# A gated cross-attention block on one core: layer norm on an input transposed by the host, and work moved from VectorE to ScalarE

## The reference

```
q = layernorm(x); k = v = ctx                       # 256 x 512
gates = [q, k, v] @ [igate_kernel, fgate_kernel] + bias   # 8 input, 8 forget gates a token
per head (8 heads of 64): D from cumulated log-sigmoid of the forget gates and a running maximum,
   C = (q @ k.T / 8) * D, h = C / (max(|sum C|, exp(-max)) + eps) @ v, then an RMS norm
x = x + tanh(g_xattn) * h
t = layernorm(x)                                    # second norm
g, u = bitlinear(t, w_gate), bitlinear(t, w_up)     # 2048 wide, tokens and weights quantised
x = x + tanh(g_ffn) * bitlinear(relu(g)**2 * u, w_down)
```

## Time and profile before

| | |
|---|---|
| median of 3 runs | 602.35 us (601.4 to 603.7) |
| the profiled execution | 605.11 us, its span 603.4 us |
| PE busy | 578.3 us, 96% |
| DVE busy | 526.2 us, 87% |
| ACT busy | 453.1 us, 75% |
| POOL busy | 129.9 us, 22% |
| granted TensorE clock, mean | 0.986 |

### The profile page before, as it was taken

The page is one execution under the profiler, slowest core; times in us unless marked ns, Lnnn a source line. Parts: engine busy times, 40 slices in busy tenths (PEclk is TensorE's granted clock), DMA queues, the critical chain, the costliest instruction groups (busy, mean ns, idle before and its releaser), DMA issues.

```text
span 603.4 us, 18384 instructions
## 1 busy us (share of the span) xinstructions
PE 578.3 (96%) x6571; PEld 339.0 (56%) x6571; DVE 526.2 (87%) x1150; ACT 453.1 (75%) x926; POOL 129.9 (22%) x284
## 2 busy tenths in 40 slices
PE   7986779999999999999999999999999999999996
PEld 3744435656565655656565655656565655655452
DVE  3799897998989898998989898998989898997964
ACT  4799888686876868686886869687786868687661
POOL 3267142120311212120211213120221213120100
PEclk9999879999999999999999999999999999999998
DMA  9959050050605023050504023050504114020100
GB/s 315 382 194 316 28 174 21 23 189 4 211 0 190 20 92 117 18 192 0 210 0 172 37 77 132 18 192 0 197 12 143 66 43 168 20 89 1 37 18 35
DMA packets 44114, 62.68 MB, mean 104 GB/s; under 512 B 1849, under 2 KB 25649, under 8 KB 44081
## 3 DMA queue, kind: packets, MB, share of 16 engines
q1 hardware_dynamic: 44080, 62.24, 29.6%
HBM read 53.72 MB, written 8.51 MB: 103 GB/s over the span
## 4 chain that ended last, share of the span: by engine, by line
PE 81%; ACT 8%; DVE 5%; issue 4%; POOL 1%; DMA 1%; SPq 0%; DVEq 0%; ACTq 0%; POOLq 0%
PE yb L1230 17%; PE gb L1204 17%; PE ub L1204 16%; PE tp L1251 8%; PE ab L1238 7%; PE ab L1218 4%; PE tp L1278 3%; PE ab L1261 3%; PE ab L1239 2%; ACT wdT L528 1%; ACT wgT L536 1%; POOL stage L446 1%; PE ab L1312 1%; DVE stage L810 1%; DMA xs<-in_x 1%
## 5 line engine op out<-in xcount | busy, mean ns | idle before, releaser
L1204 PE MATMUL gb<-wgT,xqT 128*128 128x512 bf16 x512 | 133.6, 384 | 0.0
L1204 PE MATMUL ub<-wuT,xqT 128*128 128x512 bf16 x512 | 132.6, 382 | 0.5 <-DVE stage L810 0.3
L1230 PE MATMUL yb<-wdT,stage 128*128 128x512 bf16 x512 | 124.0, 387 | 4.2 <-ACT stage L558 4.2
L544 ACT ACTIVATE relu<-gb 128x512 f32<-128x512 f32 x128 | 75.3, 588 | 45.9 <-PE gb L1204 45.5
L810 DVE TENSOR_TENSOR stage<-relu,ub 128x512 f32<-128x512 f32 x128 | 86.9, 679 | 16.2 <-ACT relu L546 16.2
L1204 PEld LDWEIGHTS ub<-wuT,xqT 128*128 128x128 bf16 x512 | 49.5, 98 | 63.5 <-DVE stage L810 4.8
L546 ACT ACTIVATE relu<-relu 128x512 f32<-128x512 f32 x128 | 80.8, 631 | 4.1
L937 DVE SCALAR_TENSOR_TENSOR dmat<-ab,dmat 128x384 f32<-128x384 f32 x128 | 65.1, 550 | 19.3 <-POOL dmat L454 13.3
L1230 PEld LDWEIGHTS yb<-wdT,stage 128*128 128x128 bf16 x512 | 47.8, 99 | 54.6 <-issue 5.0
L1204 PEld LDWEIGHTS gb<-wgT,xqT 128*128 128x128 bf16 x512 | 46.1, 101 | 45.4 <-issue 1.9
L454 POOL TENSOR_SCALAR_AFFINE_SELECT dmat<-dmat 128x256 f32<-128x256 f32 x128 | 55.7, 463 | 59.5 <-ACT dmat L604 46.8
(11 more groups left out here) (131 smaller groups left out, 893.7 us busy)
## 6 DMA issues: line engine op xcount, KB each, us to landing
dmat<-max_rows SPq DMA_DIRECT2D x15, 1024.0 KB, 5.1
values<-in_ctx_v SPq DMA_DIRECT2D x16, 520.0 KB, 7.6
xs<-in_x SPq DMA_DIRECT2D x16, 512.0 KB, 5.9
cT<-in_ctx_t SPq DMA_DIRECT2D x16, 512.0 KB, 6.9
out<-stage SPq DMA_DIRECT2D x32, 256.0 KB, 2.0
stage<-in_w_gate SPq DMA_DIRECT2D x4, 1024.0 KB, 12.1
stage<-in_w_up SPq DMA_DIRECT2D x4, 1024.0 KB, 13.5
stage<-in_w_down SPq DMA_DIRECT2D x4, 1024.0 KB, 7.1
```

Source lines behind the costliest of these rows:

```text
L544: nc.scalar.activation(relu[:, c % 2, :], gb[c % 2][:, :], ACT.Relu).then_inc(g_free, 1)
L1204: last = nc.tensor.matmul(bank[c % 2][:, :], xqT[par][:, t, d, :], w[:, d, c * CH:(c + 1) * CH], start=(d == 0), stop=(d == KD - 1))
L1230: done = nc.tensor.matmul(yb[:, :], hqT[:, c, :], wdT[:, c, :], start=(c == 0), stop=(c == KF - 1))
```

## The change

Before, x was normalised on VectorE (two tensor_scalar), transposed on TensorE (eight transposes) and copied to `qT` on ScalarE. Now the host also hands over x transposed, and one more transfer of 512 KB a batch (`turned`) puts it into `qT`. Means and reciprocal deviations lie one to a partition; TensorE transposes each of the four columns, broadcast to 128 x 128, into the bank `yb`, so that every partition there holds them as rows (`stat_rows`), and VectorE subtracts and multiplies them in place (`norm_rows`, four tensor_tensor). Batches 0 and 1 keep the old way. Since `yb` is in use, `down(b-1, 1)` now starts only after `norm_rows`.

The token centres of the second norm (x2 less its mean, now with the sign turned) go from VectorE to ScalarE, before the rstd operations. The second half of both evictions of quantised hidden transposes goes from VectorE to ScalarE in the steps from 1 to 13; `hidden(b, 1, 1)` moves ahead of the token maxima. For the last batch `down` is made in two halves of 256 columns, with two outputs and two stores, and in the last step the hidden maximum of tile 1 is split after 2 chunks instead of 3. Eight more matmuls keep TensorE busy in the prologue.

```diff
+            def turned(n, par):
+                sp.dma_start(qT[par][:, :, :], x_t[bass.ds(n, 1), :, :].rearrange("o (k p) s -> p (o k) s", p=P)).then_inc(xt_in[par], 16)
             def load(n, par):
                 for t in range(T):
                     sp.wait_ge(x2_ready[t], n - 1)
                 queries(n, par)
+                turned(n, par)
...
+            def token_centres(n, npar):
+                act.wait_ge(ln2_step, LN2_K * n + 4)
+                for t in range(T):
+                    nc.scalar.activation(xm[:, t, :], x2[npar][:, t, :], ACT.Identity, scale=-1.0,
+                                         bias=mv2[:, t, 0:1]).then_inc(centred, 1)
...
@@ ScalarE, the steps @@
+                    hidden_cols(b - 1, 1, 1)
                 if n is not None:
                     heads(n, 3)
                     squares(n)
-                if m is not None:
-                    for t in range(T):
-                        columns(m, qT[par], t)
                 quantise_high(b, 0)
...
+                    token_centres(n, npar)
                     tokens_rstd(n)
                 if m is not None:
                     hidden_cols(b, 0)
+                if prev and m is not None:
+                    hidden_cols(b, 0, 1)
...
@@ VectorE @@
+            def norm_rows(m, par):
+                dve.wait_ge(rows_full, m - 1)
+                dve.wait_ge(xt_in[par], turned_loads(m, par))
+                halves = [qT[par][:, :, t * P:(t + 1) * P] for t in range(T)]
+                for t in range(T):
+                    mean_row = yb[:, None, t * P:(t + 1) * P].to_broadcast([P, KD, P])
+                    nc.vector.tensor_tensor(halves[t], halves[t], mean_row, ALU.subtract).then_inc(q_step, 1)
+                for t in range(T):
+                    rstd_row = yb[:, None, S + t * P:S + (t + 1) * P].to_broadcast([P, KD, P])
+                    dve.wait_ge(q_step, 2 * m - 3 + t)
+                    nc.vector.tensor_tensor(halves[t], halves[t], rstd_row, ALU.mult).then_inc(q_ready, 1)
...
-                    attention_norm(m, par)
+                    norm_rows(m, par)
                 hidden_max(b, 0, 0)
                 if not prev:
                     magnitudes(2, 3)
                 hidden(b, 0, 3)
-                if prev and n is not None:
-                    hidden_cols(b - 1, 1)
...
                     scale_weight(2, 2)
                 elif m is not None:
                     hidden(b, 1, 0)
-                if n is not None:
-                    token_centres(n, npar)
+                if prev:
+                    hidden(b, 1, 1)
+                if n is not None:
+                    token_maxima(n)
                 if not prev:
                     scale_weight(2, 3)
+                if n is not None:
+                    quantise_tokens(n)
+                if n is None:
+                    hidden_max(b, 1, 0, NC // 2)
+                if not prev or m is None:
+                    hidden_cols(b, 0)
+                hidden(b, 1, 2)
+                if m is not None:
+                    negated_max(m)
+                if n is not None:
+                    hidden_max(b, 1, 0)
+                hidden(b, 1, 3)
+                if n is not None:
+                    hidden_max(b, 1, 1)
                 else:
-                    hidden(b, 1, 1)
-                if n is not None:
-                    quantise_tokens(n)
-                hidden_cols(b, 0)
-                hidden(b, 1, 2)
-                if m is not None:
-                    negated_max(m)
-                hidden_max(b, 1, 0)
-                hidden(b, 1, 3)
-                hidden_max(b, 1, 1)
+                    hidden_max(b, 1, 1, NC // 2)
...
+            for e, bank in enumerate((yb, gb[0])):
+                cols = slice(D // 2 * e, D // 2 * (e + 1))
+                dve.wait_ge(y_full, 2 * B + e)
+                if e == 0:
+                    dve.wait_ge(dq_ready, 2 * B)
+                    dve.wait_ge(out_done[1], 16 * LAST)
+                nc.vector.scalar_tensor_tensor(ot[1][:, cols], bank[:, cols], dq[:, 1:2], x2[LAST % 2][:, 1, cols],
+                                               ALU.mult, ALU.add).then_inc(o_ready, 1)
...
@@ TensorE @@
+                    if c == 0 and m is not None:
+                        pe.wait_ge(q_ready, Q_K * (m + 1))
...
+            def stat_rows(b, m):
+                pe.wait_ge(rstd_step, RSTD_K * (m + 1))
+                pe.wait_ge(stat_step, STAT_K * (m + 1))
+                if at(b, 0):
+                    pe.wait_ge(winv_step, WSUM[1])
+                else:
+                    pe.wait_ge(o_ready, 2 * b - 1)
+                alone(pe, pe_passed)
+                for i, stat in enumerate((mv[:, 0, 0:1], mv[:, 1, 0:1], rstd[:, 0:1], rstd[:, 1:2])):
+                    last = nc.tensor.transpose(yb[:, i * P:(i + 1) * P], stat.to_broadcast([P, P]), ident[:, :])
+                last.then_inc(rows_full, 1)
...
+                    stat_rows(b, m)
                 if n is None:
                     hidden_transposes(b - 1, 1)
                 chunk(b, 0, 3, par)
...
-                    q_columns(m, par)
                 if prev:
-                    down(b - 1, 1, 0, KF // 2)
+                    down(b - 1, 1, 0, KF // 2, m)
                 if m is not None:
                     gate_products(m, par, 0, 2 * T * KD)
...
-            down(LAST, 1, 0, KF)
+            pe.wait_ge(o_ready, 2 * LAST + 1)
+            pe.wait_ge(g_free, 8 * LAST + 7)
+            for e, bank in enumerate((yb, gb[0])):
+                cols = slice(D // 2 * e, D // 2 * (e + 1))
+                for c in range(KF):
+                    if e == 0 and c % (KF // 2) == 0:
+                        pe.wait_ge(a_free[c // (KF // 2)], hidden_use(LAST, 1) + 1)
+                    done = nc.tensor.matmul(bank[:, cols], hqT[:, c, :], wdT[:, c, cols], start=(c == 0), stop=(c == KF - 1))
+                done.then_inc(y_full, 1)
```

More of the change, by code:

```diff
@@ L30, with gated_block @@
 GATE_TILES = 4
-def gated_block(nc, x, ctx_t, ctx_v, small_in, w_gate, w_up, w_down, max_rows, out):
+def gated_block(nc, x, x_t, ctx_t, ctx_v, small_in, w_gate, w_up, w_down, max_rows, out):
     B, S, D = x.shape
@@ L176, in gated_block @@
         x_in = [sem(f"x_in{i}") for i in range(2)]
+        xt_in = [sem(f"xt_in{i}") for i in range(2)]
         ct_in = [sem(f"ct_in{i}") for i in range(2)]
@@ L182, in gated_block @@
         q_ready = sem("q_ready")
+        rows_full = sem("rows_full")
+        q_step = sem("q_step")
+        centred = sem("centred")
         tp_full = sem("tp_full")
@@ L289, in head_use, with turned_loads @@
             return row_use("head", n, p)
+        def turned_loads(n, par):
+            return 8 * (n - par)
         def loads_of(n, par):
@@ L407, in _ @@
             schedule(sp, step)
-            store(LAST, 1)
+            for e in range(2):
+                cols = slice(D // 2 * e, D // 2 * (e + 1))
+                sp.wait_ge(o_ready, 2 * B + e)
+                sp.dma_start(out[LAST:B, P:S, cols].rearrange("o p d -> p (o d)"), ot[1][:, cols]).then_inc(out_done[1], 16)
             for t in range(T):
-                sp.wait_ge(out_done[t], 16 * B)
+                sp.wait_ge(out_done[t], 16 * (B + t))
         @block.gpsimd
@@ L551, in columns, with hidden_cols @@
                                      ab[t][:, :].rearrange("p (k s) -> p k s", s=P), ACT.Copy).then_inc(a_free[t], 1)
-            def hidden_cols(b, t):
+            def hidden_cols(b, t, e=0):
                 if not (at(b, 0) and t == 0):
                     act.wait_ge(y_full, 2 * b + t)
-                act.wait_ge(a_full[0], hidden_use(b, t) + 1)
-                nc.scalar.activation(hqT[:, 0:KF // 2, :], abh[0].rearrange("p (k s) -> p k s", s=P), ACT.Copy,
-                                     bias=-MAGIC16).then_inc(a_free[0], 1)
+                act.wait_ge(a_full[e], hidden_use(b, t) + 1)
+                nc.scalar.activation(hqT[:, e * KF // 2:(e + 1) * KF // 2, :], abh[e].rearrange("p (k s) -> p k s", s=P), ACT.Copy,
+                                     bias=-MAGIC16).then_inc(a_free[e], 1)
             def quantise_high(b, t):
@@ L675, in _ @@
             magnitudes(1, 2, 4)
+            token_centres(0, 0)
             tokens_rstd(0)
@@ L768, in _ @@
             quantise_high(LAST, 1)
-            hidden_cols(LAST, 1)
+            act.wait_ge(y_full, 2 * LAST + 1)
+            act.wait_ge(a_full[1], hidden_use(LAST, 1) + 1)
+            nc.scalar.activation(hqT[:, KF // 2:KF, :], abh[1].rearrange("p (k s) -> p k s", s=P), ACT.Copy,
+                                 bias=-MAGIC16).then_inc(a_free[1], 1)
         @block.vector
@@ L998, in token_stats, with token_maxima @@
                     nc.vector.bn_aggr(mv2[:, t, :], st2[:, t, :]).then_inc(ln2_step, 1)
-            def token_centres(n, npar):
+            def token_maxima(n):
                 k = LN2_K * n
                 for t in range(T):
[L1003 to L1006, removed]
```

(14 more changed lines are left out.)

43 lines of the change are left out of this document (22 added, 21 removed).

## The result

| | time, median | |
|---|---|---|
| before | 603.03 us | 601.40 to 605.05 |
| changed | 629.06 us | 628.77 to 629.52, 4 runs |
| ratio | 1.0434 | 95% interval 1.0413 to 1.0456 |

The change makes the kernel 4.3% slower; forecast were 626.8 us and 611 to 636. The profiled execution took 629.52 us, its span 627.8 us; the forecast for it was 629.5.

The account below looks back on a forecast made before the run. A loop TensorE, ScalarE, VectorE, TensorE, as long as TensorE's own work, was taken to bound the kernel. Thirteen turns +22.0, start +3.9, end -1.5 sum to +24.4: 629.5 us profiled, 626.8 median; range 611 to 636.

Parts of the forecast that it names:

- The turn: One step, from a start of `down(b, 0)` to the next: from 34.17 to 35.86 us, bounds +0.97 and +2.17.
- the old slack of 0.45: Spare time on ScalarE between the end of eviction L558 and the start of `down`: 0.45 us before the change.
- the centres' term: Token centres on ScalarE, between the moments and the eviction `down` waits for: 1.20 us, against 0.45 of slack.
- The product operations: Four tensor_tensor of `norm_rows` on VectorE, at L810's pace of 0.60 each: 2.40 us, bounds 1.82 and 2.76.
- The pair of centres: Two token-centre activations on ScalarE over 512 elements: between 1.06 and 1.32 us, taken at 1.20.
- The transposes with a broadcast operand: Four on TensorE before `chunk(b, 0, 3)`, at 0.15 each: 0.61 us, between nothing and 1.22.
- VectorE's stretch: VectorE's part of the loop, up to the product that frees `ub`: no slack, net +0.89 us, bounds +0.31 and +1.25.
- TensorE's waits: Per turn, 2.3 us: about 1.1 at `cumulative_sum` for logf, 0.4 in `chunk(b, 1, 2)`, 0.8 before `down`.
- the last matmuls: Sixteen at the kernel's end, 5.31 us at clock 0.68, become 32 of half width: +0 to 1 us.
- Rival 1: TensorE sets the step, as its busy total says, and gains 0.61 us a step: 596 us in all; 9%.
- Rival 2: Only VectorE's delay of +0.89 us a turn counts and ScalarE's centres are hidden: 616 us in all; 13%.
- Rival 3: New waits also lower TensorE's clock, eight matmuls per step at 1.2 GHz: 23 us more, 650 in all; 7%.

Follow-up runs that it names:

- e3: Changed kernel with the token centres back on VectorE, behind `hidden(b, 1, 1)` and ahead of the token maxima: 618.20 us, ratio 1.0256.
- e1: Changed kernel with the eviction that `down(b, 0)` waits for put ahead of the token centres on ScalarE: 618.72 us, ratio 1.0273.
- e2: Changed kernel with the old first norm back; centres and second evictions stay on ScalarE: 616.01 us, ratio 1.0223.
- e4: Changed kernel with centres and second evictions back on VectorE, leaving only the new first norm and the end: 636.81 us, ratio 1.0562.
- e12: Changed kernel with `norm_rows` spread over the step, centres on VectorE, and `heads(n, 3)` between ScalarE's two evictions of b-1: 599.68 us, ratio 0.9937.
- e11: e4 plus four matmuls with unused results in TensorE's wait for logf, steps 1 to 13: 623.99 us, ratio 1.0343.
- e8: Changed kernel with old norm and centres on VectorE, keeping only the second evictions on ScalarE and the end: 603.95 us, ratio 1.0006.

## Why the prediction was right

**The mechanism.** The turn was forecast at 35.86 and is 36.08. From the first of the norm's operations to the end of the moments VectorE takes 1.11 us more than before (360.37 to 339.66 + 36.08, against 344.09 to 324.18 + 34.17); 0.89 was forecast. The centres add 1.24 on ScalarE, of which the old slack of 0.45 is taken off: 0.79; 1.11 + 0.79 = 1.90, the measured turn is 1.91 longer. The removals bear the centres' term out: without them on ScalarE's stretch the turn is 0.71 (e3) or 0.82 (e1) shorter, 0.83 and 0.87 in the mean of twelve. For the norm the direction is shown and the size less well: without it the turn is 1.01 shorter (e2), where 1.5 was expected. The rows of e2 put the rest down to the new wait for `heads(n, 3)` and to TensorE's 0.24.

**The terms.** The product operations were taken at 0.60, and four take 2.39. That choice decided the size of the turn: at 0.455, the pace of the operations removed, the turn would have been 0.58 shorter. The Trainium skill, "VectorE: DVE Perf Modes", section "The perf-mode tier table", puts an fp32 tensor_tensor at the base rate. The trace agrees in that the four run at the pace of the product (0.60) and not at that of the tensor_scalar (0.455). The pair of centres was taken at 1.20 and takes 1.24. The estimate after the Trainium skill, "ScalarE: Activation LUTs", section "What ACT_TABLE_LOAD costs", was 1.24, and the trace agrees with it. The transposes with a broadcast operand take about 0.5, not 0.61; TensorE waits in this turn, so nothing hangs on it.

**What was missed in the turn.** 0.22 us: I took the eviction off VectorE's stretch at its pace of 0.60. But it stood between a product and the maximum that reads it, and part of it cost nothing there. It is worth 0.38 (the maximum starts 1.19 after its product before, 347.86 less 346.67, and 0.81 now).

**TensorE's waits.** Forecast: 1.1 for logf, 0.4 for `ub`, 0.8 for `down`, 2.3 together; measured 1.39, 0.23 and 0.76, together 2.38.

**Start and end.** `down(0, 0)` starts 3.7 later (87.97), 3.9 were forecast. The end (from the start of `down(13, 0)`) is 3.3 shorter, 68.96 against 72.3, where I had 1.5. The forecast also counted thirteen turns of 34.17: there are twelve, and the one ahead of them, from `down(0, 0)` to `down(1, 0)`, took 36.85 before and 38.00 now. At the end the mis-sized term is that of the last matmuls, which I had at +0 to 1: they gain 1.63, as their clock no longer falls. Altogether: 3.7 + 1.1 (that first turn) + 12 x 1.91 - 3.3 = 24.4 in the span, as measured and as forecast. The two misses, 2.0 us too little over the turns and 1.8 at the end, cancel by luck: the total is nearer than the terms deserve.

**The rivals.** Rival 1 (TensorE's share of 96% is what counts) falls with TensorE's 2.38 us of waits. Rival 2 (the centres are hidden) falls with e1 and e3. Two more that the change suggests show no wait in the turn: VectorE has no idle time before `norm_rows` at 360.37, so x transposed had landed, and `norm_rows` ends at 362.76, before TensorE is done with the heads (363.24, 0.92 us) and comes to `down(b-1, 1)`. Rival 3 does not hold for the changed kernel, whose turns run at 1.00, but its mechanism is real and sits close by: e4 loses 1.5 us to it in most turns. I had no measured bound between waits that cost clock and waits that do not, and the 1.39 here is not far from the 1.76 there.

**What stays open.** Why the changed kernel keeps the full clock with waits of 1.39, 0.23 and 0.76 us, and why e4 loses it after ten of its waits of about 1.76 and keeps it after three that are as long: the length of the wait alone does not decide it, and no run varies it in steps. Why the clock holds at the end of the changed kernel, where the waits are shorter, was not tested either. Nor was it tried whether filling the 0.21 us gap before the maximum would help e12.

## What to carry to other kernels

When two engines are as full as this, take one loop of waits (here from one `down` to the next), and book each moved operation on the stretch where it stands: an operation added to a stretch without slack costs its full pace, and one taken off the fuller engine elsewhere gives nothing (e3: VectorE busier, the turn shorter). Moving work off an engine also moves the work behind it on the other: ask of each instruction that now stands behind the newcomer (`heads(n, 3)` here) who waits for it. The same exchange of two instructions can be worth half a microsecond a turn or cost more than that, depending on who needs the bank next.

## What the runs showed of the hardware

- The product of 512 fp32 elements and the maximum that reads its result start 0.81 us apart on VectorE (changed kernel, 0.82 in e2 and e12); before the change an eviction that does not read it started 0.59 after the product. That eviction, whose pace is 0.60, put the maximum off by only 0.38.
- In e4, waits of TensorE of 1.75 to 2.15 us, one in a turn, were followed by 5.2 us at a granted clock of 0.67 ten times of thirteen (a mean that holds the lower level, 1.2 GHz, for most of the stretch) and by 1.00 three times. With four unused matmuls in that place (e11) the turn ran at 1.00. At the end, waits of 1.35 and 0.82 before and after the 16 transposes went with 0.68 before the change, waits of 0.65 and 0.43 with 1.00 after it, and 0.79 and 0.43 with 1.00 in e8.
- A stationary operand that is one column broadcast with stride 0 costs a transpose no more than a full tile: about 0.5 us for four (359.08 to 359.55), 1.22 for eight full ones (347.33 to 348.55 before the change).
